# A transformer block on one core: four waits and a statistics step put at other places in the queues

## The reference

```python
def xattn(query, ctx):                       # 16 heads of 32
    Q, K, V = query @ Wq.T + bq, ctx @ Wk.T + bk, ctx @ Wv.T + bv
    qk = einsum('bhqd,bhkd->bhqk', Q, K)
    scores = qk / sqrt(32)
    feats = [scores.mean((-2, -1)), scores.max(-1).mean(-1),
             var(softmax(scores), -1, ddof=1).mean(-1)]        # per head
    t = exp(clip(mlp(feats), log 0.1, log 10))                 # 3 -> 64 -> 64 -> 1, gelu
    return softmax(qk / (2 * t)) @ V @ Wo.T + bo

def ffn(x):                                  # 512 -> 2048 -> 512
    h = gelu(quant_act(x) @ ternary(w1).T)
    return quant_act(h) @ ternary(w2).T      # quant_act: per row, to 8 bits

x = x + tanh(g_xattn) * xattn(layernorm(x), ctx)
x = x + tanh(g_ffn) * ffn(layernorm(x))
```

## Time and profile before

| | us |
|---|---|
| median of 3 runs | 1305.19 (1303.17 to 1305.79) |
| the profiled execution | 1306.91 |
| its span, first to last instruction | 1305.1 |
| TensorE busy | 1178.8 (90%) |
| VectorE busy | 1074.5 (82%) |
| ScalarE busy | 946.4 (73%) |
| GpSimd busy | 424.0 (32%) |

### The profile page before, as it was taken

One profiled execution on the slowest core, in us unless ns is written; L12 is line 12 of the kernel. 1 busy time (PEld: TensorE's weight loads), 2 busy tenths in 40 slices (PEclk: granted clock), 3 DMA queues, 4 the chain that ended last, 5 costly groups with the idle time before them and its releaser, 6 DMA issues.

```text
span 1305.1 us, 19199 instructions
## 1 busy us (share of the span) xinstructions
PE 1178.8 (90%) x6684; PEld 439.4 (34%) x6684; DVE 1074.5 (82%) x1969; ACT 946.4 (73%) x1593; POOL 424.0 (32%) x489
## 2 busy tenths in 40 slices
PE   4866599999999999999999999999999999969988
PEld 2322212444224432344224431344224431224224
DVE  7789789887898889887998879887898879984256
ACT  4678689566985689575985779765985769765833
POOL 3138554420453224530363224511363201120210
PEclk9869789999999999999999999999999999979989
DMA  8722111211112221202112221102212210001000
GB/s 313 224 80 66 44 54 49 50 43 55 33 49 49 58 74 49 49 17 58 57 50 49 50 81 49 29 21 66 65 49 49 50 65 1 1 1 65 1 1 33
DMA packets 36017, 73.35 MB, mean 56 GB/s; under 512 B 8145, under 2 KB 8529, under 8 KB 35409
## 3 DMA queue, kind: packets, MB, share of 16 engines
q1 hardware_dynamic: 35920, 72.13, 19.3%
HBM read 38.39 MB, written 8.39 MB: 36 GB/s over the span
## 4 chain that ended last, share of the span: by engine, by line
PE 65%; DVE 19%; ACT 6%; issue 4%; SPq 3%; DMA 2%; POOL 1%; DVEq 0%; ACTq 0%; POOLq 0%
PE b_ps L1459 10%; DVE nmax L1013 7%; PE b_ps L1491 6%; PE o_ps L1697 6%; PE z_ps L1515 6%; PE o_ps L1504 6%; DVE stat L1023 5%; PE o_ps L1459 5%; PE z_ps L1459 5%; PE a_ps L1485 5%; PE b_ps L1663 4%; PE z_ps L1697 2%; ACT region L815 2%; PE z_ps L1663 2%; PE o_ps L1663 2%
## 5 line engine op out<-in xcount | busy, mean ns | idle before, releaser
L783 ACT ACTIVATE etile<-a_ps,nmax 128x512 f32<-128x512 f32 x512 | 351.7, 702 | 81.9 <-DVE nmax L1013 80.9
L1013 DVE TENSOR_REDUCE nmax<-a_ps 128x1 f32<-128x512 f32 x512 | 345.2, 679 | 57.0 <-PE a_ps L1485 55.3
L815 ACT ACTIVATE region<-b_ps,inv2t 128x512 f32<-128x512 f32 x512 | 335.0, 704 | 47.1 <-PE b_ps L1491 43.3
L1023 DVE BATCH_NORM_STATS2 stat<-etile 128x6 f32<-128x512 f32 x492 | 335.1, 683 | 13.2 <-ACT etile L783 13.1
L1485 PE MATMUL a_ps<-kst,qst 96*128 96x512 f16 x512 | 197.0, 392 | 32.6 <-ACT etile L783 25.4
L1491 PE MATMUL b_ps<-qst,kst 97*128 97x512 f16 x512 | 193.7, 388 | 11.3 <-ACT region L957 5.7
L1504 PE MATMUL o_ps<-region,vbuf 128*32 128x512 f32 x1024 | 137.2, 607 | 15.0 <-DVE region L1051 8.7
L1515 PE MATMUL z_ps<-region,ones 128*32 128x512 f32 x1024 | 136.5, 605 | 8.1 <-DVE region L1054 8.1
L682 POOL TENSOR_TENSOR region<-region 128x512 f16<-128x512 f32 x64 | 77.5, 1210 | 195.9 <-ACT region L858 195.4
L1491 PEld LDWEIGHTS b_ps<-qst,kst 97*128 97x128 f16 x512 | 49.6, 97 | 251.4 <-ACT region L815 202.0
L590 POOL TENSOR_TENSOR region<-region 128x512 f32<-128x512 f32 x32 | 40.8, 1276 | 258.3 <-DVE region L1061 258.3
(11 more groups left out here) (332 smaller groups left out, 1993.2 us busy)
## 6 DMA issues: line engine op xcount, KB each, us to landing
kst<-region SPq DMA_DIRECT2D x96, 128.0 KB, 2.3
qst<-region SPq DMA_DIRECT2D x84, 128.0 KB, 2.3
xres<-in_x_dram SPq DMA_DIRECT2D x8, 1024.0 KB, 5.4
out_dram<-xres SPq DMA_DIRECT2D x32, 256.0 KB, 2.0
cin<-in_ctxT_dram SPq DMA_DIRECT2D x30, 256.0 KB, 2.8
cin<-in_x_dram SPq DMA_DIRECT2D x28, 256.0 KB, 2.6
kst<-in_f1T_dram SPq DMA_DIRECT2D x2, 1024.0 KB, 8.6
qst<-in_f2T_dram SPq DMA_DIRECT2D x2, 1024.0 KB, 9.2
```

Of the source, the lines that this page charges most:

```text
L783: nc.scalar.activation(etile[:, k % E_SLOTS, :], a_ps[k % A_BANKS][:, :], ACT.Exp, bias=nmax[:, slot_of(n), t:t + 1], scale=1.0, accum_out ...
L815: nc.scalar.activation(probs[:, (s + 1) % 2, g, :], b_ps[g % 2][:, :], ACT.Exp, scale=inv2t[:, slot:slot + 1]).then_inc(b_exp, 1)
L1013: vec.tensor_reduce(nmax[:, slot_of(k // T), k % T:k % T + 1], a_ps[k % A_BANKS][:, :], AX.X, ALU.max, negate=True).then_inc(a_max, 1)
L1023: vec.bn_stats(stat[:, slot_of(k // T) * T + k % T, :], etile[:, k % E_SLOTS, :]).then_inc(a_stat, covered)
```

## The change

It moves waits and one step in the engines' orders; no arithmetic changes.

- `X_STATS_AT`: VectorE runs `stat_x` of pair 0 at the end of set 9, not of set 8.
- The waits of TensorE for ScalarE's copies of V tiles 0 to 2, in front of the Q products, go to the turn of t = 1 in full bodies, beside the one for tile 3.
- `early(0)` leaves its place between `turn(3)` and `down(2)` and goes into the middle of `down(2)`, behind its eighth matmul (bodies 1 to 7).
- The transpose of the maxima waits for `a_max`; the wait for `feat_done` follows behind it, in front of the first product of the small network.

```diff
--- before.py
+++ after.py
@@ -53,7 +53,7 @@
 A_PLAN_7 = (48, (3, 3, 3, 3, 2, 2, 0, 0, 0, 0, 0, 0, 0, 0, 0, 0))
 
 X_ORDER = (2, 3, 0, 1)
-X_STATS_AT = (8, 13)
+X_STATS_AT = (9, 13)
 NORM_AT = ((0, 3), (1, 0), (1, 2))
 A_BANKS, E_SLOTS, E_LATE, S_LATE = 4, 3, 1, 2
 EARLY = 6
@@ -1638,7 +1638,7 @@
                 if has_p:
                     for t in range(T):
                         drained(i, "X", t)
-                        if not first and (t < T - 1 or not has_b):
+                        if not first and not has_b:
                             drained(i, "V", t)
                 for n in range(C):
                     cols = slice(n * P, (n + 1) * P)
@@ -1692,8 +1692,8 @@
                     drained(i, f"turn{t}", 1)
                     bank_n = take(i, f"down{t}")
                     for k in range(KC):
-                        if t == T - 1 and k == KC // 2 and has_a:
-                            early(2)
+                        if t >= T - 2 and k == KC // 2 and has_a:
+                            early(0 if t == T - 2 else 2)
                         ins = mat(mm_ps[bank_n][:, :], hT[t % 2][:, k, :], f2[:, k, :], start=k == 0, stop=k == KC - 1)
                     ins.then_inc(mm_full[bank_n], 1)
 
@@ -1714,10 +1714,8 @@
                 for t in range(T):
                     if has_b:
                         turn(t)
-                        if t == 1 and has_p:
-                            drained(i, "V", T - 1)
-                        if t == T - 1 and has_a:
-                            early(0)
+                        for row in range(T) if t == 1 and has_p else ():
+                            drained(i, "V", row)
                         if t > 0:
                             down(t - 1)
                         if t + 2 < T:
@@ -1726,11 +1724,12 @@
                         if i == 0:
                             pe.wait_ge(setup_dve, SETUP_STEPS)
                             pe.wait_ge(kst_ones, 32)
-                        pe.wait_ge(feat_done, nth(i, 1, 1))
+                        pe.wait_ge(a_max, nth(i, H * T, H * T))
                         bank_n = take(i, "M", 0)
                         nc.tensor.transpose(mm_ps[bank_n][0:H * T, 0:P], nmax[:, :, :].rearrange("p h t -> p (h t)"),
                                             ident32[:, :]).then_inc(mm_full[bank_n], 1)
                         bank_n = take(i, "M", 1)
+                        pe.wait_ge(feat_done, nth(i, 1, 1))
                         for f in range(3):
                             ins = mat(mm_ps[bank_n][0:DH, 0:H], w1r[:, f, :], feat[:, f, :], start=f == 0,
                                       stop=f == 2)
```

## The result

The changed kernel takes 1324.55 us (median of 5 runs, 1321.96 to 1326.7) against 1305.19 (1303.17 to 1305.94) for the kernel before, run beside it on the same chip. The ratio is 1.0146, with a 95% interval of 1.0135 to 1.0157: slower by about 19 us. Forecast were 1319 us, in a range of 1306 to 1327. The profiled execution took 1324.55 us, its span is 1322.5 us, and the mean granted clock of TensorE is 0.955 (before 0.966).

The account below looks back on a forecast made before the run. The last-ending chain was taken as two thirds TensorE, a fifth VectorE. Terms +14.7 + 10.2 - 2.4 - 8.3 = +14.2 on 1306.9 us gave 1321, set to 1319 for the median of runs; range 1306 to 1327.

Parts of the forecast that it names:

- The chain on GpSimd is late: Bodies 1 to 6: later statistics delay GpSimd's split_y, so VectorE's part 0 of group 2 stands some 3.9 us.
- Rival C: VectorE's part 0 of group 2: GpSimd's chain not late, -1.43 us a body instead of +2.45; 1286 us, chance 0.15.
- Its price in the loop: Set loop of bodies 1 to 6: 2.45 us later each, removed z-product stall already counted; +14.7 us.
- The clock: TensorE behind its 4.3 us gap, bodies 1 to 6: clock falls to 1.2 GHz, 1.7 us each, +10.2 us.
- rival B: Set loop: the new wait comes but TensorE's clock stays at 2.4 GHz; 1309 us (1306 to 1312), chance 0.18.
- V and the early scores: V waits before Q products: 0.4 us in six bodies; gap before early scores: 1.18 us in seven; -2.4 and -8.3 us.
- The V term: Before the Q products, bodies 1 to 6: of 0.9 us waits only 0.4 us arrives, -2.4 us in all.
- rival D: Wait and low clock come, but ScalarE and VectorE take back the gains at turn and V; 1330 us, chance 0.11.
- The maxima: Transpose of the maxima, body 0: comes earlier, but SP's queue delays the row; some 0.3 us off the chain, taken 0.
- rival A: As computed, new wait and low clock in the loop: 1319 us (1313 to 1326), chance 0.56.

Follow-up runs that it names:

- experiment 4: Changed kernel with split_y of group 1 before normalise_x in GpSimd's queue: 1288.97 us; with pair 1's statistics also in set 14, 1286.85 us.
- experiment 1: Kernel before with only X_STATS_AT changed from (8, 13) to (9, 13): 1333.0 us, ratio 1.0212.
- experiment 3: Changed kernel with one second score of set 13 repeated 18 times on TensorE to fill the gap, bodies 1 to 6: 1309.52 us.
- experiment 5: Changed kernel with split_y of group 1 between the two split_x on GpSimd and statistics in sets 9 and 14: 1308.83 us, ratio 1.0031.
- experiment 2: Changed kernel with X_STATS_AT put back to (8, 13), the other three edits kept: 1295.16 us, ratio to before 0.9921.
- `y_first_14`: Changed kernel with split_y of group 1 before normalise_x on GpSimd and X_STATS_AT at (9, 14): 1286.85 us, ratio 0.9861.

## Why the prediction was right, point by point

**The chain on GpSimd is late.** Right, in each number of its working. The prediction put the statistics' end at 357.51 and the new part 0 at 369.7; body 2's set loop starts 353.27 - 351.74 = 1.53 us later in the new trace, and less that the measured events are at 357.5 and 369.70. VectorE stands 3.78 us (3.9 forecast), TensorE 4.34 (4.3 forecast). That it is the order on GpSimd, and not its work, is shown by experiment 4: the same instructions in another order cost nothing. Rival C, a chain that is not late, falls.

**Its price in the loop.** 15.2 us against 14.7. Five bodies show 2.47 us instead of 2.45; one, body 3, shows 2.83, because VectorE waits 4.1 us there. Experiments 1, 3 and 5 have it too, each in body 3. GpSimd's instructions there take no longer; the time lies behind the last of them, which ends at 523.95, while VectorE goes on only at 524.41, 0.46 us later. In body 2 it was 0.11 us (371.12 to 371.23). What holds VectorE for the other 0.35 us is not settled.

**The clock.** Right in that it falls, so rival B, with the clock kept, falls too; experiment 3, with the gap filled, shows what B would have been (1309.5 measured, 1309 worked out for it). The term was under-sized: 2.17 us a body, 13.0 in all, not 1.7 and 10.2. The step that was off is the time until the clock comes back. It was read from two places of body 0, 4.9 and 2.8 us after work resumed, and the middle, 3.9, was taken. In the loop it is 3.0 to 6.3 us, 4.8 in the mean of the six bodies: in body 3 the clock is back at about 528.2, 3.0 us after the restart at 525.25, in body 2 after 6.0. The loss is half of that time less 0.1 to 0.3 us, 1.37 and 2.75 us in these two; so the 0.2 left for what hides was fair. The bound of 2.4 per body was passed in bodies 2 and 5 (2.75 and 2.91), not by the mean.
The Trainium skill, page "TensorE: Matmul & The Clock Gate", section "Why this matters for your kernels", advises against idle gaps beyond some 3 us between bursts of matmuls. The gap of 4.34 us agrees with it. Experiment 5 has gaps of 2.56 us, shorter than that figure, that cost the clock as well; there the measurement decides.

**V and the early scores.** The rest of the body is 92.44 - 90.91 = 1.53 us shorter, against 0.4 + 1.18 = 1.58; apart they measure 0.4 and 1.1. The V term was bounded by ScalarE's copy two steps on, and that is where 4.0 of 5.4 us went. The early scores come where the prediction put them, 0.5 us later than before: 2.64 us behind the transposes against 2.10. They hold nothing up (all engines, end of body 2):

```profile
465.22 1.07 PE L1674 MATMUL b_ps<-ident,region 128*128 128x128 f16 x16
466.13 1.89 PE L1697 MATMUL o_ps<-f,region 128*128 128x512 fp8e4 x8
467.86 0.38 PE L1491 MATMUL b_ps<-qst,kst 97*128 97x512 f16 x1
...
468.46 0.17 DVE L1202 TENSOR_SCALAR inv2t<-expt 128x16 f32<-128x16 f32 x1 [1.44 <-ACT expt L985]
...
468.72 1.26 ACT L815 ACTIVATE region<-b_ps,inv2t 128x512 f32<-128x512 f32 x2 [0.29 <-PE b_ps L1491]
```

The first score is there at 468.24 and the temperature at 468.63, and the exponent starts 0.09 us after the temperature, as it did before (313.09 to 313.18). So rival D, in which these gains are given back, falls with experiment 2.

**The maxima.** Nothing, as said. The row of maxima is copied early, but SP's queue sends it last, as the earlier trace rows let expect:

```profile
153.81 7.48 SPq L442 DMA_DIRECT2D qst<-region  x12
161.34 0.59 SPq L490 DMA_DIRECT2D qst<-mrow  x1
```

**The sum.** From the forecast's +14.2 to the measured +17.4 of the span: the wait +0.5, the clock +2.8, V and early scores of six bodies +0.4, the start-up -1.5, and bodies 7 and 8 +0.9 (the early scores do give 1.15 us there, something else in these bodies takes most of it back, and that it is low-clock stretches at other places is not shown). What is left to 1324.55, about 2 us, is the step from the profiled execution down to the median of the runs: 1.7 us were taken off for it, and the changed kernel's profiled execution lies on its median. So the mechanism was right and the forecast 5.5 us low, half of that by the clock term; that it was no lower is partly luck, for the start-up gave 1.5 us back that no term had. The upper end of rival A, 1326, comes out with the clock's bound and no gain at V; with the bound given for the early scores (-4.8 for -8.3) it would be 1329. Why low-clock stretches in bodies 0, 7 and 8 move between kernels stays open. For the 1.5 us in the start-up no edit was found: the same place, 187.7 before and 186.2 after, is at 186.53 in experiment 1, which changes nothing in front of it, at 185.77 in `y_first_14` and at 187.92 in experiment 5. So one trace of each kernel doesn't show this to be an effect of the change.

## What to carry to other kernels

When a step is moved on one engine, list what the engine that waits for it has queued behind the wait, and who waits for the last of these: here the moved statistics were needed by nobody soon, but the y buffer behind them was, and another order on GpSimd (with the second pair's statistics a set later) turns 27.6 us of loss into a gain of 8. A gap of TensorE in a dense loop costs its length and then half of the time until the granted clock is back (here 1.4 to 2.9 us on a gap of 4.3); to tell the two apart, fill the gap with matmuls that are thrown away. Where one edit of several is bad, run each by itself: the good parts were worth 10 us and were hidden under it.

## What the runs showed of the hardware that was not expected

A gap of 2.6 us was enough. In experiment 5 the clock fell in six bodies of six, and in bodies 2 to 6 only after work had resumed, 0.2 to 1.1 us after (body 5: work goes on at 819.55, the clock falls at about 820.4). In the kernel before, TensorE had two gaps of nearly that length in body 0 and stayed at full clock through both:

```profile
101.18 0.39 PE L1485 MATMUL a_ps<-kst,qst 96*128 96x512 f16 x1 [2.50 <-ACT etile L783]
...
107.86 0.39 PE L1485 MATMUL a_ps<-kst,qst 96*128 96x512 f16 x1 [2.50 <-ACT etile L783]
```

```profile
98.00:102.00 4.00, 1.50 (x8) 0.41 (x5) 4.00 (x4) 3.60 (x7) 3.91 (x3) 1.00 0.00 0
...
106.00:110.00 4.00, 1.26 (x5) 0.41 (x5) 3.97 (x7) 2.06 (x6) 2.08 (x3) 1.00 0.16 51
```

But neither the length of the gap nor the work close around it decides this. The clock fell at about 110.0, 2.2 us after the second of them. And the first of the two is in the changed kernel's trace as well, with the same length and the same work around it (1.50 us of the 4 from 98 to 102 in both traces). There the clock fell 0.7 to 0.8 us after it:

```profile
100.83 0.39 PE L1485 MATMUL a_ps<-kst,qst 96*128 96x512 f16 x1 [2.50 <-ACT etile L783]
```

```profile
101.00:102.00 1.00, 1.00 (x5) 0.23 (x4) 1.00 (x3) 0.83 (x2) 0.92 (x1) 0.79 0.00 0
102.00:103.00 1.00, 1.00 (x4) 0.40 (x4) 1.00 (x3) 1.00 (x4) 0.92 (x3) 0.50 0.00 0
```

So here a gap of 2.5 us cost the clock in one trace and not in another; the expectation of experiment 5 went by the one in which it did not. Rival B rested on the idea that gaps in a dense stretch are the harmless ones; these runs speak against it. For body 5 of experiment 5, two windows:

```profile
819.00:820.00 1.00, 0.45 (x5) 0.19 (x8) 1.00 (x3) 0.00 (x0) 0.92 (x2) 1.00 0.00 0
820.00:821.00 1.00, 1.00 (x9) 0.13 (x2) 1.00 (x2) 0.00 (x0) 0.40 (x1) 0.68 0.06 16
```

And the time until the clock is back is not fixed: behind the same gap of 4.34 us the second stretch of the loop took from 12.14 to 13.50 us in one execution of the changed kernel, and 12.48 to 12.61 in one of experiment 1. Which body gets which could not be foretold from the gap.
